# Combine loops of a fused network kernel: the residual, or the norm's scaling and turn, behind the tree of sums

## The reference, cut to what matters

```python
x = x + 0.5 * _L0_ffn_ref(_layernorm(x), ...)     # routed experts
x = x + _L0_attn_ref(_layernorm(x), ...)          # a selective scan
x = x + 0.5 * _L0_ffn_ref(_layernorm(x), ...)
x = x + 0.5 * _L1_ffn_ref(_layernorm(x), ...)     # first soft stage, s = 0
x = x + _L1_attn_ref(_layernorm(x), ...)          # gated linear attention
x = x + 0.5 * _L1_ffn_ref(_layernorm(x), ...)     # second soft stage, s = 1
```

```python
def _L1_ffn_ref(x, phi_w, phi_b, expert_w, expert_b):     # 64 experts, 32 slots each: 2048 slots
    logits = (jnp.einsum('tzd,ed->tze', x, phi_w) + phi_b).reshape(t, z, n, p)
    D = jax.nn.softmax(logits, axis=3)        # over the slots of an expert: dispatch
    C = jax.nn.softmax(logits, axis=2)        # over the experts: combine
    X_tilde = jnp.einsum('tznp,tzd->npd', D, x)
    ...
    Y_tilde = jnp.einsum('npd,ndH->npH', X_tilde, expert_w) + expert_b[:, None, :]
    Y = jnp.einsum('tznp,npH->tzH', C, Y_tilde)
    return Y

def _layernorm(x, axis=-1, eps=1e-05):
    m = jnp.mean(x, axis=axis, keepdims=True)
    v = jnp.var(x, axis=axis, keepdims=True)
    return (x - m) / jnp.sqrt(v + eps)
```

## Time and profile before

| | |
|---|---|
| median of 3 runs | 2232.11 us (2231.87 to 2232.35) |
| profiled execution | 2253.2 us |
| its span, first to last instruction | 2251.4 us |
| PE busy | 1869.9 us (83%) |
| DVE busy | 1666.6 us (74%) |
| ACT busy | 1184.8 us (53%) |
| POOL busy | 1230.3 us (55%) |
| first soft stage's combine, loop | from about 1355 to 1545 us of the span |
| second soft stage's combine, loop | from about 2038 to 2222 us of the span |

### The profile page before, as it was taken

How to read it: one execution, slowest core, us unless ns; L and a number is a source line. 1 busy time by engine, 2 the same in 40 slices (tenths; PEclk the granted TensorE clock), 3 DMA queues, 4 the chain that set the end, 5 groups by cost and what they waited for, 6 DMA issues and landing times.

```text
span 2251.4 us, 24417 instructions
## 1 busy us (share of the span) xinstructions
PE 1869.9 (83%) x6046; PEld 907.8 (40%) x6046; DVE 1666.6 (74%) x2166; ACT 1184.8 (53%) x2820; POOL 1230.3 (55%) x796
## 2 busy tenths in 40 slices
PE   4099686888888833986999999998987999999998
PEld 3067532333333521764333344443333433344443
DVE  5223488999999840327999967886687999958886
ACT  2322186555555332215999854332456999963332
POOL 3734307999999564552999800000785999900000
PEclk9999898999999956998999999999899999999999
DMA  7123293455455111325000000000650300000000
GB/s 261 50 84 103 94 154 113 169 178 176 169 176 176 64 60 51 107 71 169 1 0 0 1 1 1 0 0 0 186 141 19 94 0 0 0 1 5 9 9 14
DMA packets 102320, 163.63 MB, mean 73 GB/s; under 512 B 11008, under 2 KB 65843, under 8 KB 102113
## 3 DMA queue, kind: packets, MB, share of 16 engines
q1 hardware_dynamic: 94050, 146.41, 22.0%
q0 software_dynamic: 8192, 16.30, 2.0%
HBM read 125.09 MB, written 38.14 MB: 73 GB/s over the span
## 4 chain that ended last, share of the span: by engine, by line
PE 35%; DVE 32%; issue 15%; POOL 9%; ACT 4%; DMA 2%; another core or an unknown queue 1%; DVEq 1%; POOLq 0%; SPq 0%; ACTq 0%
PE ps L2005 10%; DVE arena L1461 5%; PE ps L1737 5%; PE ps L1750 5%; DVE arena L1523 5%; DVE arena L1467 5%; DVE arena L1459 4%; PE ps L1876 4%; PE ps L2033 3%; POOL arena L575 2%; POOL arena L638 2%; DVE arena L1529 2%; DVE arena L1406 2%; DVE stage L1156 2%; POOL arena L600 1%
## 5 line engine op out<-in xcount | busy, mean ns | idle before, releaser
L1951 PE MATMUL ps<-arena 128*128 128x512 f32 x512 | 250.6, 612 | 13.9 <-POOL arena L600 13.8
L608 POOL TENSOR_TENSOR arena<-arena 128x864 f32<-128x864 f32 x128 | 210.1, 1642 | 80.2 <-DVE arena L1459 77.4
L1942 PE MATMUL ps<-c_phiT,arena 128*128 128x512 f32 x512 | 244.1, 600 | 5.8 <-DVE arena L1461 3.8
L2005 PE MATMUL ps<-XT,c_phiT 128*128 (+1 forms) x512 | 243.4, 593 | 3.9 <-DVE arena L1499 3.9
L600 POOL TENSOR_TENSOR arena<-arena 128x1024 f32<-128x1024 f32 x128 | 246.6, 1928 | 0.0
L2033 PE MATMUL ps<-arena 128*128 128x512 f32 x512 | 227.7, 604 | 11.2 <-DVE arena L1529 11.2
L638 POOL TENSOR_TENSOR arena<-arena 128x1024 f32<-128x1024 f32 x32 | 63.6, 2000 | 299.2 <-DMA arena<-value_rows 299.2
L538 POOL DMA_INDIRECT token_outputs<-arena x128 | 124.3, 971 | 151.0 <-DVE arena L1298 112.0
L889 ACT ACTIVATE arena<-arena 128x32 f32<-128x32 f32 x640 | 195.7, 311 | 0.0
L1406 DVE TENSOR_TENSOR_SCAN arena<-ps,arena 128x1024 f32<-128x1024 f32 x84 | 187.9, 2274 | 6.4 <-POOL arena L570 6.2
L1876 PE MATMUL ps<-arena,c_ident 128*128 128x512 f32 x336 | 161.0, 601 | 28.3 <-POOL arena L575 28.3
(11 more groups left out here) (241 smaller groups left out, 3711.7 us busy)
## 6 DMA issues: line engine op xcount, KB each, us to landing
arena<-input_gates SPq DMA_DIRECT2D x128, 512.0 KB, 3.8
arena<-value_rows SPq DMA_DIRECT2D x32, 512.0 KB, 5.0
arena<-slot_inputs SPq DMA_DIRECT2D x32, 258.0 KB
arena<-in_L_ffn_w SPq DMA_DIRECT2D x32, 256.0 KB
arena<-token_outputs SPq DMA_DIRECT2D x16, 512.0 KB, 6.7
slot_inputs<-arena SPq DMA_DIRECT2D x1, 4128.0 KB, 13.4
slot_inputs<-zero SPq DMA_DIRECT2D x1, 4128.0 KB, 33.5
token_outputs<-arena SPq DMA_DIRECT2D x1, 4096.0 KB
```

Source lines behind the costliest of these rows:

```text
L608: pool.tensor_tensor(Ed[:, r, PSLOT * NA:].rearrange("p (n q) -> p n q", q=PSLOT), Lc[:, r, PSLOT * NA:].rearrange("p (n q) -> p n q", q=P ...
L1942: ins = pe.matmul(pbank(2 * h + c), xts[:, r // 2, :], phiT[:, at:at + CHUNK], start=True, stop=True)
L1951: ins = pe.matmul(pbank(4 + 2 * h + c), xns[:, r // 2, :], Dd[:, r, CHUNK * c:CHUNK * (c + 1)], start=start, stop=stop, skip_group_check=True)
L2005: ins = pe.matmul(pbank(t % 4), phiT[:, P * t:P * (t + 1)], xt(b, c), start=True, stop=without_m)
```

## The change

In the loop's body DVE does the second half of `weigh` and the tree ahead of `ln_apply` (first stage) or `residual` (second stage). PE does `ln_turn` after `total` and `turn_y`, and ACT does `finish` ahead of `ln_copies`. The norm's statistics of this stage (n = 4) go to two fixed places of `stats` and `ln_s`, one for each parity of the chunk (`ring`), whose addresses are constants; so `bn_aggr` serves inside the loop too, and the seven small operations go. `ln_step` counts one for a chunk everywhere.

```diff
@@ scalar, ln_scale
-            def ln_scale(n, c):
+            def ln_scale(n, c, ring=None):
+                at = 4 * (c if ring is None else ring)
                 hold(act, sem("ln_var"), 8 * n + c + 1)
-                act.activation(ln_s[:, 6, ds(4 * c, 4)], ln_s[:, 5, ds(4 * c, 4)], ACT.Ln, bias=eps[:, :])...
+                act.activation(ln_s[:, 6, at:at + 4], ln_s[:, 5, at:at + 4], ACT.Ln, bias=eps[:, :])...
...
@@ scalar, loop
                         copy_y(v - 1)
+                        finish(v)
                         if s == 0:
                             ln_copies(4, i - 1, c, 7)
-                        finish(v)
@@ vector, ln_statistics
                 for j in range(PER_CHUNK):
-                    ins = dve.bn_stats(stats[:, ds(4 * c + j, 1), :]..., X[:, ds(4 * c + j, 1), :]...)
-                if isinstance(v, int):
-                    ins.then_inc(sem("ln_step"), 3)
-                    dve.wait_ge(sem("ln_step"), 3 * v + 3)
-                    for t in range(4 * c, 4 * c + 4):
-                        ins = dve.bn_aggr(ln_s[:, 4:6, t], stats[:, t, :])
-                    ins.then_inc(sem("ln_var"), 1)
-                    return
+                    ins = dve.bn_stats(stats[:, at + j, :], X[:, ds(4 * c + j, 1), :]...)
                 ins.then_inc(sem("ln_step"), 1)
-                dve.wait_ge(sem("ln_step"), 3 * v + 1)
...
+                hold(dve, sem("ln_step"), 8 * n + c + 1)
+                for t in range(at, at + PER_CHUNK):
+                    ins = dve.bn_aggr(ln_s[:, 4:6, t], stats[:, t, :])
+                ins.then_inc(sem("ln_var"), 1)
@@ vector, ln_apply
+                at = 4 * (h if n == 4 else c)
                 for j in range(PER_CHUNK):
-                                            ln_s[:, 4, ds(t, 1)], ln_s[:, 7, ds(t, 1)], ALU.subtract, ALU.mult)
+                                            ln_s[:, 4, at + j:at + j + 1], ln_s[:, 7, at + j:at + j + 1], ALU.subtract, ALU.mult)
@@ vector, loop
                         less_m(v, c)
+                        weigh(v - 1, 1 - c, 1)
+                        tree(v, c)
                         if s == 0:
                             ln_apply(4, 2 * (i - 1) + c, c)
                         else:
                             residual(v - 2, i - 1, c)
-                        weigh(v - 1, 1 - c, 1)
-                        tree(v, c)
@@ tensor, loop
                         combine(v - 1, 1 - c, False)
+                        total(v)
+                        turn_y(v - 1, False)
                         if s == 0:
                             ln_turn(4, 2 * (i - 1) + c, c, 7)
-                        total(v)
-                        turn_y(v - 1, False)
```

More of the change, by code:

```diff
@@ L672, in _ @@
             act.preload_act_table_set("natural_log_exp_and_others")
-            def ln_scale(n, c):
+            def ln_scale(n, c, ring=None):
+                at = 4 * (c if ring is None else ring)
                 hold(act, sem("ln_var"), 8 * n + c + 1)
-                act.activation(ln_s[:, 6, ds(4 * c, 4)], ln_s[:, 5, ds(4 * c, 4)], ACT.Ln, bias=eps[:, :]).then_inc(sem("ln_ln"), 1)
+                act.activation(ln_s[:, 6, at:at + 4], ln_s[:, 5, at:at + 4], ACT.Ln, bias=eps[:, :]).then_inc(sem("ln_ln"), 1)
                 hold(act, sem("ln_ln"), 8 * n + c + 1)
-                act.activation(ln_s[:, 7, ds(4 * c, 4)], ln_s[:, 6, ds(4 * c, 4)], ACT.Exp, scale=-0.5)\
+                act.activation(ln_s[:, 7, at:at + 4], ln_s[:, 6, at:at + 4], ACT.Exp, scale=-0.5)\
                     .then_inc(sem("ln_rstd"), 1)
@@ L933, in exp_T @@
                         if before and t == ST - 4:
-                            ln_scale(4, 2 * before[0] + before[1])
+                            ln_scale(4, 2 * before[0] + before[1], before[1])
                         hold(act, sem("LT"), ST * v + t + 1)
@@ L968, in soft @@
                         copy_y(v - 1)
+                        finish(v)
                         if s == 0:
                             ln_copies(4, i - 1, c, 7)
-                        finish(v)
                 if s == 0:
-                    ln_scale(4, CHUNKS - 2)
+                    ln_scale(4, CHUNKS - 2, 0)
                 copy_y(base + CHUNKS - 1)
@@ L976, in soft @@
                     ln_copies(4, BATCH - 1, 0, 7)
-                    ln_scale(4, CHUNKS - 1)
+                    ln_scale(4, CHUNKS - 1, 1)
                     ln_copies(4, BATCH - 1, 1, 7)
@@ L1118, in _, with ln_statistics @@
             chain(dve.memset(XT[:, :, 0:CONV_PAD], 0.0))
-            def ln_statistics(n, c):
-                v = 8 * n + c
+            def ln_statistics(n, c, ring=None):
+                at = 4 * (c if ring is None else ring)
                 for j in range(PER_CHUNK):
-                    ins = dve.bn_stats(stats[:, ds(4 * c + j, 1), :].rearrange("p a b -> p (a b)"),
-                                       X[:, ds(4 * c + j, 1), :].rearrange("p a b -> p (a b)"))
-                if isinstance(v, int):
-                    ins.then_inc(sem("ln_step"), 3)
-                    dve.wait_ge(sem("ln_step"), 3 * v + 3)
-                    for t in range(4 * c, 4 * c + 4):
-                        ins = dve.bn_aggr(ln_s[:, 4:6, t], stats[:, t, :])
-                    ins.then_inc(sem("ln_var"), 1)
-                    return
-                ins.then_inc(sem("ln_step"), 1)
-                dve.wait_ge(sem("ln_step"), 3 * v + 1)
[L1135 to L1145, removed]
+                    ins = dve.bn_stats(stats[:, at + j, :], X[:, ds(4 * c + j, 1), :].rearrange("p a b -> p (a b)"))
+                ins.then_inc(sem("ln_step"), 1)
+                hold(dve, sem("ln_step"), 8 * n + c + 1)
+                for t in range(at, at + PER_CHUNK):
+                    ins = dve.bn_aggr(ln_s[:, 4:6, t], stats[:, t, :])
+                ins.then_inc(sem("ln_var"), 1)
             def ln_apply(n, c, h):
@@ L1153, in ln_apply @@
                         dve.wait_ge(sem("ln_keep"), 8 * KEPT.index(n) + c - 1)
+                at = 4 * (h if n == 4 else c)
                 for j in range(PER_CHUNK):
-                    t = 4 * c + j
-                    ins = dve.tensor_scalar(stage[:, h, D * j:D * (j + 1)], X[:, ds(t, 1), :].rearrange("p a d -> p (a d)"),
-                                            ln_s[:, 4, ds(t, 1)], ln_s[:, 7, ds(t, 1)], ALU.subtract, ALU.mult)
+                    ins = dve.tensor_scalar(stage[:, h, D * j:D * (j + 1)], X[:, ds(4 * c + j, 1), :].rearrange("p a d -> p (a d)"),
+                                            ln_s[:, 4, at + j:at + j + 1], ln_s[:, 7, at + j:at + j + 1], ALU.subtract, ALU.mult)
                 ins.then_inc(sem("ln_x"), 1)
@@ L1538, in residual @@
                         dve.wait_ge(sem("s_add"), v + 1)
-                        ln_statistics(4, 2 * i2 + c)
+                        ln_statistics(4, 2 * i2 + c, c)
                 def less_m(v, c):
```

## The result

The changed kernel takes 2227.57 us in the median of 20 runs (2225.59 to 2231.41), the kernel before 2233.85 in the median of 20 (2230.89 to 2236.52). The ratio is 0.9976, 95% interval [0.997, 0.9982], so 5.4 us less by the ratio (4.0 to 6.7); the two medians are 6.3 apart. Forecast was 7.6 less, a time of 2224.5 in a range of 2221.5 to 2228.5: the sign and the range held, the size was about 2 us too good. The exponential of `finish` on ACT is L952.

The account below looks back on a forecast made before the run. A cycle from `total` through `turn_y`, logits, `less_m`, `ln_apply` or `residual`, `weigh` and the tree was taken to bound both combine loops; -4.0 and -3.6 us sum to -7.6, from 2232.11 to 2224.5 us, range 2221.5 to 2228.5.

Parts of the forecast that it names:

- Second loop, -3.6: Second combine loop: `residual` behind the tree lets the tree start 0.60 us earlier in each of six units, -3.6 us.
- Both margins, `s_add` and the copy of yT: Second loop: `turn_y` waits for both, and both end before it begins, `s_add` with 0.4 us to spare; no cost.
- First loop, VectorE, -6.18: First combine loop: `ln_apply` behind the tree takes 1.03 us off each of six units, -6.18 us.
- First loop, TensorE, +2.15: First combine loop: `ln_turn` behind `total` and `turn_y` delays the logits by 0.43 us in five units, +2.15 us.
- ScalarE's copies, nothing: First loop: `ln_copies` behind `finish` fits before the first exponential, due 3.3 us after `total`; no cost.
- Statistics, nothing: First loop: the new form takes 1.9 us, 1.0 less, but the saving is off the cycle; no gain.
- The clock, 3 us both ways: Last combine behind each loop, partly at lower clock: a shift can change its length, 3 us either way in the range.
- 1 (all of the first loop's gain given back): First loop's restart misses its small margins, leaving only the second loop's 3.6 us: 2228.5 us, chance 0.11.
- 2 (the turn waits): First loop: `ln_turn` waits for a late `ln_apply` and holds PE; with 3 us a unit, 2239.5 us, chance 0.03.
- 3: Both loops: PE is bound by its own work and the 0.69 us wait is not real; 2232 us, chance 0.03.

Follow-up runs that it names:

- a2: Kernel before with only the second stage's `residual` moved behind the tree: ratio to the kernel before 0.9979, second loop 181.25 us.
- b2: Changed kernel with VectorE's loop order of before, PE's turn and ACT's copies left late: first loop 193.44 us, no ratio taken.
- b3: Changed kernel with `ln_turn` back ahead of `total` and `ln_copies` ahead of `finish`, `ln_apply` still behind the tree: first loop 193.91 us, no ratio taken.
- c1: Changed kernel plus 45 unused memsets on VectorE, putting its second dispatch loop back at position 1887: ratio to the kernel before 0.9966.
- a4: Changed kernel with the old order on all three engines, keeping only the new statistics: ratio to the kernel before 1.0009, first loop 191.25 us.

## Why the prediction was right, and what it missed

- *Second loop, -3.6:* right. 3.5 measured in the changed kernel and alone (a2). Both margins, `s_add` and the copy of yT, held; no wait appeared ahead of `turn_y`.
- *First loop, VectorE, -6.18:* right, as part of -4.08. The loop's branch fits the rest of the hole: the units with and without it are 31.29 and 31.30 us.
- *First loop, TensorE, +2.15:* right; b2 measures it alone, 193.44 - 191.25 = 2.2 us. b3 shows that it can't be avoided by leaving the turn ahead of `total`.
- *ScalarE's copies, nothing:* right. The logits resume 0.43 behind the turn, and the first exponential is 3.2 us behind `total` (forecast 3.3).
- *Statistics, nothing:* this is the step that missed, by place and not by size. In the loop they do cost nothing (0.1 us gained; the form itself takes 1.36 us where 1.9 was estimated). But they take 44 instructions out of VectorE's program, and the dispatch loop behind them then runs 0.20 us slower a pass, 2.9 us in all. The forecast priced instructions where they run and took code that isn't edited as fixed. With the old place restored (c1) the ratio is 0.9966 (0.9954 to 0.9978), and the forecast was 2224.5 / 2232.11 = 0.9966. That the two agree to the last digit is luck, since the interval is 5 us wide and the dispatch's start and the clock moved by about 1 us each; that the loops sum to 7.6 again is not.
- *The clock, 3 us both ways:* it moved, by less. The last combine of the second stage takes 15.66 us after, and 17.04 and 17.00 in the two profiles of the kernel before. In the changed kernel's windows the granted clock is 0.63 over the one in which that combine starts (at 2205.08), a mean of the two levels 1.2 and 2.4 GHz, and 1.00 (2.4 GHz) in the next; the last three figures are the granted clock, the DMA share and GB/s:

```profile
2204.00:2210.00 6.00, 4.92 (x8) 2.23 (x9) 5.87 (x3) 0.00 (x0) 0.00 (x0) 0.63 0.00 0
2210.00:2216.00 6.00, 6.00 (x16) 2.65 (x15) 0.00 (x0) 0.00 (x0) 0.00 (x0) 1.00 0.17 46
```

Over all kernels this combine takes 15.36 (a2) to 17.04 us, one profile each; a4, whose second loop is that of before, has 15.59. So these profiles don't show that the new order shortened it, and whether it explains the 4.7 of a2, where the loop gave 3.5, is not shown either: a2's interval takes in both. The Trainium skill, "TensorE: Matmul & The Clock Gate", Part 1, says that the same kernel can show a different number of cold matmuls from run to run. The first stage's last combine agrees, with 16.13 and 15.76 us in the two profiles of the kernel before; the second stage's, 17.04 and 17.00, hardly varied.
- *Rivals:* 1 (all of the first loop's gain given back) did not happen: the loop kept it. 2 (the turn waits) is what b3 shows, in another order, at 1.12 us a unit. 3 is out.

Account of the changed kernel: -4.08 - 3.51 + 2.9 = -4.7; measured -5.4 (-4.0 to -6.7). In the profiles the stretch behind the second loop is 1.4 us shorter besides (28.99 to 27.57), which would give -6.1. So the time came into the range with a loss of 2.9 us that the forecast didn't have and a gain at the clock that it had only as play: that they partly offset each other is luck, and without the gain the size would have been missed by more.

What stays open: why the place makes the passes of one loop 14.48, 14.59 or 14.68 us long. That it has to do with how VectorE fetches its code is a guess. Five places were seen (1887; 1845, 1847, 1855; 1843), too few for a rule, and the place was not varied by itself beyond these.

## What to carry to other kernels

Find the cycle of a pipelined loop by following the releases once around, then move work that nobody awaits into an engine's wait for the far end of the cycle; the price is read from start-to-start times, and in these two loops it came out to 0.1 us. Before moving a producer, look at its consumer on another engine: if that stands ahead of what the cycle waits for, as in b3, it has to move too. And when an edit changes the length of an engine's code, look at the later loops of that engine that it did not touch: compare the length of each loop before believing a total.

## What the runs showed of the hardware that I had not expected

The same VectorE loop of 31 instructions with the same data and neighbours takes 14.48 us a pass at position 1887 of the program, 14.59 to 14.60 at 1845, 1847 and 1855, and 14.68 at 1843. The difference lies between the last instruction of a pass and the first of the next (0.48 us against 0.60 to 0.61), and at 1843 there is a second loss of 0.08 two units on. Memsets that nothing reads, run once (0.86 us, 150 us earlier), bring the short passes back: the dispatch falls from 240.89 to 238.73 us, 2.2 less.
